# Cross-partition maxima, sums and score vectors of a four-layer graph kernel turned in 32 by 32 blocks on VectorE instead of on TensorE

## The reference, cut to what matters

```python
# x: [1354, 256], adj: [1354, 1354], all float32
x = layernorm(x + relu(adj @ (max(sign(x), 0) @ sign(W0).T)))        # L0: binary layer
# L1: edge layer
h = x @ W_sa
scores = (h @ a_sa[0, :256])[:, None] + (h @ a_sa[0, 256:])[None, :] # left scores, right scores
e = where(adj != 0, exp(-leaky_relu(scores, 0.01)), 0)
x = layernorm(x + sigmoid(attn_a * (e / (e.sum(1) + 1e-5)) @ h + attn_b * (adj @ (x @ W_gcn) + b)))
x = layernorm(x + (adj != 0) @ (x @ W + b) / deg)                    # L2: mean layer
y = x                                                                # L3: two softmax layers
for l in range(2):
    Wh, Ws = split(y @ W_stack[l])
    y = leaky_relu((softmax(Wh @ Ws.T, -1) * adj) @ Wh + y, 0.01)
out = layernorm(x + y)
```

## Time and profile before

| | |
|---|---|
| median of 3 runs | 483.96 us |
| the profiled execution | 483.51 us, of which 481.7 us is its span from first to last instruction |
| TensorE matmul busy | 471.0 us (98%), 1921 matmuls |
| VectorE busy | 349.7 us (73%) |
| ScalarE busy | 235.8 us (49%) |
| GpSimd busy | 187.4 us (39%) |
| granted TensorE clock, mean | 0.995 of full |

### The profile page before, as it was taken

The page is one execution under the profiler, slowest core; times in us unless marked ns, Lnnn a source line. Parts: engine busy times, 40 slices in busy tenths (PEclk is TensorE's granted clock), DMA queues, the critical chain, the costliest instruction groups (busy, mean ns, idle before and its releaser), DMA issues. The chain is left out here.

```text
span 481.7 us, 5723 instructions
## 1 busy us (share of the span) xinstructions
PE 471.0 (98%) x1921; PEld 310.7 (64%) x1921; DVE 349.7 (73%) x760; ACT 235.8 (49%) x417; POOL 187.4 (39%) x186
## 2 busy tenths in 40 slices
PE   8999999999999999999999999999999999999994
PEld 7999755545555688887545444554556545778882
DVE  5688799999955799748133953992853399799994
ACT  5979379973887553323434531341333376342200
POOL 1444654552352068823000631461440064356641
PEclk9999999999999999999999999999999999999998
DMA  8955310000544000000000000000000000000001
GB/s 293 291 164 178 128 33 1 0 1 0 181 165 150 1 1 0 1 0 1 1 0 0 0 1 1 1 1 0 0 0 1 0 2 1 1 11 23 22 23 39
DMA packets 8180, 20.69 MB, mean 43 GB/s; under 512 B 1008, under 2 KB 4740, under 8 KB 8152
## 3 DMA queue, kind: packets, MB, share of 16 engines
q1 hardware_dynamic: 7144, 19.02, 11.9%
q0 software_dynamic: 464, 0.79, 0.7%
q10 hardware_dynamic: 544, 0.52, 0.3%
HBM read 18.94 MB, written 1.39 MB: 42 GB/s over the span
## 5 line engine op out<-in xcount | busy, mean ns | idle before, releaser
L1505 PE MATMUL psum<-QT,xT 128*128 128x512 f32 (+3 forms) x264 | 108.5, 542 | 0.0
L427 POOL TENSOR_TENSOR es<-es,ST 128x512 f32<-128x512 f32 (+3 forms) x60 | 75.1, 1252 | 51.2 <-ACT ST L627 49.4
L622 ACT ACTIVATE ST<-psum 128x512 f32<-128x512 f32 (+3 forms) x66 | 36.1, 547 | 86.8 <-DVE rm L985 77.6
L1505 PEld LDWEIGHTS psum<-QT,xT 128*128 128x128 f32 (+1 forms) x264 | 47.7, 186 | 40.4 <-issue 34.0
L985 DVE TENSOR_TENSOR rm<-psum,rm 128x512 f32<-128x512 f32 (+3 forms) x60 | 37.4, 624 | 38.7 <-PE psum L1505 38.4
L365 POOL TENSOR_TENSOR rstd<-veps,nhalf 128x1 f32<-128x1 f32 (+1 forms) x44 | 29.3, 667 | 68.9 <-DVE veps L769 68.9
L1619 PE MATMUL psum<-Wh,ST 128*128 128x256 f32 (+3 forms) x242 | 55.1, 380 | 0.0
L1549 PE MATMUL psum<-ST,Wh 128*128 128x512 f32 (+3 forms) x132 | 54.5, 542 | 0.0
L1317 PE MATMUL psum<-eb,x_all 128*128 128x512 f32 (+3 forms) x132 | 51.9, 542 | 0.0
L627 ACT ACTIVATE ST<-ST 128x512 f32<-128x512 f32 (+3 forms) x66 | 37.9, 579 | 28.4 <-DVE ST L1007 25.5
L393 POOL TENSOR_TENSOR esumb<-esumb,eb 128x1354 f32<-128x1354 f32 (+1 forms) x10 | 32.4, 3236 | 46.8 <-ACT eb L515 46.8
(11 more groups left out here) (173 smaller groups left out, 779.3 us busy)
## 6 DMA issues: line engine op xcount, KB each, us to landing
adj_rows<-in_adj_dram SPq DMA_DIRECT2D x10, 677.0 KB, 4.9
rows<-in_adj_dram SPq DMA_DIRECT2D x10, 677.0 KB, 4.0
x_all<-in_x_dram SPq DMA_DIRECT2D x5, 256.0 KB, 4.7
out_dram<-xs SPq DMA_DIRECT2D x10, 128.0 KB, 1.7
W<-in_L_gnn_W_stack_dram SPq DMA_DIRECT2D x2, 512.0 KB, 6.3
adj_rows<-in_adj_dram SPq DMA_DIRECT2D x1, 338.5 KB
rows<-in_adj_dram SPq DMA_DIRECT2D x1, 338.5 KB
w0n<-in_L_gnn_weight_dram SPq DMA_DIRECT2D x1, 256.0 KB, 2.8
```

Of the source, the lines that this page charges most:

```text
L427: nc.gpsimd.tensor_tensor(es[0:r, g % 2, 0:w], es[0:r, g % 2, 0:w], buf(g)[0:r, j, 0:w], ALU.add)\
L622: nc.scalar.activation(buf(g)[0:r, j, 0:w], psum[0:r, SB[n % 3], 0:w], ACT.Copy).then_inc(st_ready.sem, 1)
L1505: last = nc.tensor.matmul(psum[0:r, SB[n % 3], 0:w], xT[l][:, k, j * P:j * P + r], QT[:, k, c0:c1], start=(k == 0), stop=(k == KD - 1))
```

## The change

Three spreads leave TensorE, for all but the last two groups.

- **Maxima of groups 0 to 3** (`max_blocks`): VectorE turns `rm` in 32 by 32 blocks, reduces each block, gathers the four quarters of partitions side by side with four small copies, reduces them, puts the result on the other three quarters with three copies, and turns a step-zero read of it straight into bank 7.
- **Denominators of groups 0 to 2** (`den_blocks`): the same with a sum and a reciprocal, ending in `rdb` in SBUF; ScalarE's copy goes too.
- **Left scores**: four copies gather `nsl` into `lefts`, three copies put it on the other quarters, and one block turn of a step-zero read of 1408 columns writes `nslb`; ScalarE's three copies go. They stand ahead of the right dot products.
- **`spread_dots`**: four transposes of step-zero reads of `ucol` replace eight matmul records of `Ub`; the memset and four adds of `Ub` go.

With them: ScalarE's `exp_scores(5)` moves behind the copies of `zT`; `z_proj` starts behind `h_part(2)` instead of `h_part(1)`, two for each `h_part` up to the fifth; the sums of group 1 lie in banks 5 and 6 instead of 2 and 3, so they no longer wait for `scale_t(0)`. `wh1(0)` waits for `scale_t(1)`.

```diff
+    SUMB = [2, 5, 2]
@@ ScalarE
-            for c, (c0, c1) in enumerate(CH):
-                act.wait_ge(left_spread.sem, c + 1)
-                nc.scalar.activation(nslb[:, c0:c1], bank(6 + c % 2, 0, c1 - c0), ACT.Copy).then_inc(nslb_ready.sem, 1)
...
-                exp_scores(j)
+                if j < RING - 1:
+                    exp_scores(j)
...
-                    if s == 0:
-                        rdb_evac(g)
@@ VectorE
             left_dot(T - 1)
+            dve.wait_ge(dots_done.sem, T)
+            for a in range(QUADS):
+                last = nc.vector.tensor_copy(lefts[0:BLOCK, :, a], nsl[a * BLOCK:(a + 1) * BLOCK, :])
+            own.link(last)
+            for a in range(1, QUADS):
+                last = nc.vector.tensor_copy(lefts[a * BLOCK:(a + 1) * BLOCK, :, :], lefts[0:BLOCK, :, :])
+            own.link(last)
+            nc.vector.transpose(nslb[:, :], lefts[:, :, :].rearrange("p t a -> p (t a)").unsqueeze(2).to_broadcast([P, T * QUADS, BLOCK]))\
+                .then_inc(nslb_ready.sem, 1)
...
+            def max_blocks(g):
+
+                w = chunk(g)[2]
+                nb = -(-w // BLOCK)
+                dve.wait_ge(rm_step.sem, T * (g + 1))
+                nc.vector.transpose(blocks[:, 0:nb * BLOCK], rm[:, g % 2, 0:nb * BLOCK]).then_inc(rm_blocked.sem, 1)
+                dve.wait_ge(rm_blocked.sem, g + 1)
+                own.link(nc.vector.tensor_reduce(quad[:, 0:nb], blocks[:, 0:nb * BLOCK].rearrange("p (b n) -> p b n", n=BLOCK), AX.X, ALU.max))
+                for a in range(QUADS):
+                    last = nc.vector.tensor_copy(gathered[:, a, 0:nb], quad[a * BLOCK:(a + 1) * BLOCK, 0:nb])
+                own.link(last)
+                own.link(nc.vector.tensor_reduce(quadmax[0:BLOCK, 0:nb], gathered[:, :, 0:nb].rearrange("p a b -> p b a"), AX.X, ALU.max,
+                                                 negate=True))
+                for a in range(1, QUADS):
+                    last = nc.vector.tensor_copy(quadmax[a * BLOCK:(a + 1) * BLOCK, 0:nb], quadmax[0:BLOCK, 0:nb])
+                own.link(last)
...
+                if g >= 1:
+                    dve.wait_ge(sub_done.sem, T * g)
+                nc.vector.transpose(psum[:, 7, 0:nb * BLOCK], quadmax[:, 0:nb].unsqueeze(2).to_broadcast([P, nb, BLOCK]))\
+                    .then_inc(spread_ready.sem, 1)
...
-                rden_cols(g)
+                den_blocks(g)
...
-            max_reduce(1)
+            max_blocks(1)
@@ TensorE
                 z_part(j)
-                if j == 1:
-                    for c in range(NC):
-                        spread_left(c)
...
-                for _ in range(2 if j <= 2 else 1):
-                    if i < T and j >= 1:
+                for _ in range(2 if j <= 5 else 1):
+                    if i < T and j >= 2:
                         z_proj(i)
                         i += 1
...
-                if j == T - LEAD_S:
-                    max_turn(1)
-                if j == T - 2:
-                    max_spread(1)
-            den(0)
             for s in range(LEAD_S):
                 s_tile(2, s)
-                if s == 0:
-                    spread_rden(0)
```

More of the change, by code:

```diff
@@ L528, in _ @@
             i = 0
+            exp_scores(RING - 1)
             for j in range(RING, T):
@@ L687, in _ @@
             q_evac(4)
-            wh1_evac(1)
-            rdb_evac(2)
-            for i in range(2, CROSS):
+            for i in range(1, CROSS):
                 wh1_evac(i)
@@ L1084, in _ @@
                 run_max(0, j)
-            max_reduce(0)
+            max_blocks(0)
             def both(g, s):
@@ L1109, in _ @@
                 both(0, s)
-            max_reduce(1)
+            max_blocks(1)
             turnover(0, T, 2)
-            max_reduce(2)
+            max_blocks(2)
             turnover(1, CROSS, 1)
@@ L1115, in _ @@
                 soft_step(2, s)
-            rden_cols(2)
+            den_blocks(2)
             scale_t(2)
@@ L1121, in _ @@
                 run_max(3, j)
-            max_reduce(3)
+            max_blocks(3)
             soft_step(3, 0)
@@ L1244, in spread_dots @@
                     for k in range(KD):
-                        last = nc.tensor.matmul(bank(0, half * D + k * P, half * D + (k + 1) * P), Ub[:, half, k, :],
-                                                ident[:, :], start=True, stop=True)
+                        last = nc.tensor.transpose(bank(0, half * D + k * P, half * D + (k + 1) * P), across(ucol[:, half, :], k, P), ident[:, :])
                 last.then_inc(ubc_ps.sem, 1)
@@ L1284, in z_part @@
                             last.then_inc(z_done.sem, 1)
-            def spread_left(c):
-                c0, c1 = CH[c]
-                if c == 0:
-                    pe.wait_ge(NA.x_ready.sem, T)
-                if c == 2:
-                    pe.wait_ge(nslb_ready.sem, 1)
-                for i in range(c0 // P, -(-c1 // P)):
-                    r = kk(i)
-                    pe.wait_ge(dots_done.sem, i + 1)
-                    last = nc.tensor.transpose(bank(6 + c % 2, i * P - c0, i * P - c0 + r), across(nsl, i, r), ident[0:r, 0:r])
-                last.then_inc(left_spread.sem, 1)
             def turn_exps(q):
@@ L1568, in den @@
                 last.then_inc(gat_den.sem, 1)
-            def spread_rden(g):
-                pe.wait_ge(rden_ready.sem, g + 1)
-                for n, i in enumerate(tiles(g)):
-                    r = kk(i)
-                    last = nc.tensor.transpose(bank(6, n * P, n * P + r), across(rden[:, g, :], n, r), ident[0:r, 0:r])
-                last.then_inc(rden_spread.sem, 1)
             def wh1(i):
@@ L1643, in _ @@
             q_mul(1)
-            max_turn(0)
             q_mul(2)
             s_tile(1, 0)
-            max_spread(0)
             for s in range(1, LEAD_S):
@@ L1666, in _ @@
                     s_tile(2, j + LEAD_S)
-                if j == T - LEAD_S:
-                    max_turn(2)
                 if j == T - 2:
-                    max_spread(2)
                     q_mul(3)
-            den(1)
             for s in range(LEAD_S):
                 s_tile(3, s)
-                if s == 0:
-                    spread_rden(1)
             for j in range(T):
@@ L1684, in _ @@
                     q_mul(4)
-            den(2)
-            wh1(1)
-            spread_rden(2)
-            for i in range(2, CROSS):
+            for i in range(1, CROSS):
                 wh1(i)
@@ L1692, in _ @@
             q_mul(5)
-            max_turn(3)
             wh1(CROSS)
             wh1(CROSS + 1)
-            max_spread(3)
             for j in range(T):
```

128 lines of the change are left out of this document (75 added, 53 removed).

## The result

The changed kernel takes 477.43 us (median of 4 runs, 477.12 to 478.37) for 484.01 us of the kernel before in the same comparison (4 runs, 483.92 to 484.13): a ratio of 0.9858, with 95% between 0.9841 and 0.9875. Its profiled execution took 477.23 us, of which 475.4 us is the span, for 483.51 and 481.7 before. The forecast was 477.1 with 475.5 to 480.5.

What follows compares the result with a forecast made beforehand. TensorE's streaming, busy 98% of the span, was taken as the bound. Six terms summed to 6.9 us off the profiled 483.51, giving 476.6; with 0.45 for the median, 477.1 us, range 475.5 to 480.5.

Steps and rivals of the forecast that it cites:

- left scores: Edge layer: TensorE loses its spread of the left scores, VectorE's added 3.1 us mostly hidden; gain 1.6 us, 0 to 1.5 at risk.
- spread_dots: Spreading in `spread_dots`: eight TensorE matmul records become four transposes; gain 0.4 us.
- seam of group 0: Behind group 0's last score tile: 8 transposes go, VectorE has 2.9 us in hand; gain 0.9 us.
- seam of group 1: The tight seam: 16 transposes go, but TensorE waits 0.9 to 1.5 us behind VectorE; gain 0.3 to 0.9, taken 0.5.
- seam of group 2: Behind group 2's last score tile: 14 transposes go, VectorE's 8.3 us fit in 12.0; gain 1.5 us.
- seam of group 3: `den(2)` with its spread, about 1.0, and group 3's maxima turn and spread, 1.0, leave TensorE; gain 2.0 us.
- Rival D: Whole kernel: the transposes were free and others set the pace, so nothing changes, 484.0 us; chance 0.04.
- C: Group 1 seam: VectorE not late, turns near 0.43 or copies near nothing; 1.2 us more gain, 475.5 to 475.9; chance 0.06.
- B: Group 1 seam: new wait outweighs the saving, slower; a turn of 1.65 us decides, 487.0 us at 2.0; chance 0.06.
- A: VectorE's new work: dear turns (1.26 us) or copies held by GpSimd; 480.7 us, with half of it 478.9; chance 0.18.
- the danger at `z_proj(8)`: Edge layer: `z_proj(8)` needs `zp_evac(6)`, queued on VectorE behind `scores(9)`; least cover left there about 1 us.
- The forecast's doubt: Left scores: GpSimd's `xp5` held VectorE's first score pass to 4.43 us; it would now meet the right dot products instead.

Runs made afterwards that it cites:

- e4: Changed kernel plus six redundant block turns on VectorE, two each in `max_blocks(0)`, `max_blocks(2)` and `den_blocks(1)`; 478.10 us.
- e6: Changed kernel with ScalarE's sixth exponential put ahead of the copies of `zT` again, as in the kernel before; 478.9 us.
- e5: Changed kernel with `z_proj` interleaved as in the kernel before, from `h_part(1)` on, two each up to j = 2; 477.84 us.
- e2: Changed kernel with the block sums of `den_blocks(0)` written to PSUM bank 5 and the four gathering copies reading from there; 477.41 us.
- e3: Changed kernel with two more redundant block turns of `es`, each waited for, in `den_blocks(0)`; 479.52 us.
- e8: The e3 kernel plus 20 transposes of the identity into a free PSUM bank on TensorE ahead of the waiting tile `s_tile(2, 3)`; 478.26 us.

## Why the prediction was right, and where its sum was off

Terms of the sum beside the stages, in us:

```
                   forecast   measured
left scores        1.6        1.67
spread_dots        0.4        about 0 in this execution
seam of group 0    0.9        0.88
seam of group 1    0.5        -0.09
seam of group 2    1.5        1.58
seam of group 3    2.0        2.25
sum                6.9        6.3
```

**Right, and shown.** That a transpose taken out of TensorE's full queue is worth its pace of 0.11 us: seams 0 and 2 come out within 0.1. That VectorE's block turn costs about a pass of its width: 0.70 to 0.73 for 0.69. That seam 1 is the only one where VectorE is late, that TensorE waits there for ScalarE's copy behind `run_max(2, 0)`, and that no wait appears at seams 0, 2, 3 (e4 shows that seams 0 and 2 had room for the turns of one block more). Rival D falls at once, C by the wait, B and the dear turns of A by the turns' length. The held copies of A came once, at seam 1, for 0.64; they were a sign of being wrong too ("if VectorE idles in front of copies while GpSimd runs"), and in the trace they show as a longer record (0.80 for 0.16) and not as idle time.

**Left scores.** Right in size, but with a gap in its reasons. The block took 59.06 + 1.65 - 57.49 = 3.2 us, as forecast (3.1), though made otherwise: the turn of 1408 columns was cheaper, 1.65 for 1.9, since its price doesn't grow quite with the columns (512 in 0.71, 1408 in 1.65), and the copies of `nsl` dearer, 0.2 each. The forecast looked for the danger at `z_proj(8)`; the first to suffer would have been the copies of `zT` behind an exponential on ScalarE (e6: 1.31 us). The forecast's doubt, that the hold-up by GpSimd "moves and is not new", was right for the first score pass (0.94 for 4.43) and misses that it can move to a pass that somebody waits for: the sixth tile's took 4.31 for 1.57. "What is queued behind the waiting instruction" had been asked for VectorE and not for ScalarE. The order of `z_proj` was worth another 0.6 (e5), so there was little cover.

**Seam of group 1, the step that failed.** The term was to be 0.3 to 0.9 with a wait of 0.9 to 1.5; it is -0.09 with 1.71. Three parts, all from VectorE's timeline. The hold of the copies by GpSimd was seen in the forecast (0.7) and came (0.64): that alone makes 0.3. I then took 0.5, a middle between holding and not holding, although the forecast's own schedule had the copies start inside GpSimd's addition: the hold is what is left of the addition when the first copy comes, and the schedule had given it. Second, the two blocks measure 3.79 (290.32 to 294.11) and, without the hold, 3.94 (295.31 to 299.89 less 0.64) for 3.6 and 3.8: the little reduction is 0.25 for 0.2, the reciprocal 0.24 for 0.2, and some of each. Together 0.19 + 0.14 = 0.33. Third, the restart of TensorE: 0.08, the fourth tile taking 302.17 - 300.98 = 1.19 until the next start for a pace of 1.11. 0.3 - 0.33 - 0.08 = -0.11, for -0.09 measured. A chain of ten or more small instructions, each rounded down by 0.03 to 0.05, is off by a third of a microsecond, and where the queue is on the path that all goes into the result.

**`spread_dots`.** Four matmuls fewer are there in TensorE's stream, but the start of z is at 53.88 for 53.91. In the changed kernel TensorE waits 0.6 us there for adjacency rows, which the kernel before didn't show, so what the four matmuls saved may have gone into waiting for a DMA. The stage moves by 2 us between executions, with the first DMAs and with the clock; 0.4 us can neither be confirmed nor refuted there, and no experiment was made for it.

**Seam of group 2.** The gain came as forecast, but one of its lengths was wrong: `den_blocks(1)` was put at 3.2, the length for the last chunk, while group 1 has 512 columns. VectorE's timeline of the changed kernel has its last turn, and what follows:

```profile
330.56 0.71 DVE L1066 STREAM_TRANSPOSE rdb<-quadsum 128x512 f32<-128x512 f32 x1
334.20 0.69 DVE L991 COPY rm<-psum 128x512 f32<-128x512 f32 x1 [2.93 <-PE psum L1544]
```

It began at 327.26 and so took 4.0, and the idle time of 2.93 behind it swallowed the difference; the slack there is 0.8 less than the 3.7 of the forecast.

**Seam of group 3.** 0.25 more than forecast, in two like parts. From `den(2)` to `s_tile(3, 8)` TensorE took 373.75 - 366.60 = 7.15 before and 6.04 after: 1.11 for "about 1.0". From `max_turn(3)` to `s_tile(4, 0)` it took 383.97 - 381.12 = 2.85 and 1.73: 1.12 for 1.0, of which the transposes are 0.88 and the rest a stop. In the kernel before, the eight matmuls of `wh1(8)` and `wh1(9)` between the earlier trace rows's `max_turn(3)` and `max_spread(3)` took 383.54 - 381.56 = 1.98; after the change the same eight stand thus (TensorE's timeline of the changed kernel):

```profile
375.94 1.89 PE L1615 MATMUL psum<-W,xT 128*128 128x256 f32 x8
377.67 1.88 PE L1544 MATMUL psum<-QT,xT 128*128 128x512 f32 x4
```

that is 1.73, so 0.25 of stop where the forecast had 0.12 of "small joints". `wh1(9)` writes bank 6 and had to wait there until `max_reduce(3)` had read the turned maxima (VectorE 381.76 to 382.45); the wait view leaves so short a stop out, but the distance of the starts shows it. The forecast should have looked at who else uses the bank that the removed step had occupied. That it was this wait is argued from the two timelines, not tried.

**The total.** 6.3 instead of 6.9 off the profile's span, and 477.4 instead of 477.1. Two errors of opposite sign (-0.6 and +0.25), and a term that can't be seen, lie in it. That the span came so near is in part luck: z starts at 53.91 and 53.88 in the two profiled executions, and would have been some 1.3 us apart had the clock fallen in one of them.

## What to carry to other kernels

Moving cross-partition work off a saturated TensorE pays its pace in full as long as the receiving engine's queue has nothing in it for which TensorE waits soon; cut the queue at that place and count every small instruction at its measured price, and put what isn't urgent (here the denominators) behind what is. When a producer gets later, go through every engine that waits for it and ask what is queued behind that wait: here the exponential on ScalarE, not the matmul that was guarded; ask too which passes of it now meet a neighbour that holds them. Compare stage by stage, by the starts of the same instructions, when the start of the program is noisier than the effect, and read the granted clock of the noisy stretch before calling it noise.

## What the runs showed of the hardware

- A VectorE block turn of f32 costs 0.70 to 0.73 us for 128 x 512, the same with a step-zero source and with PSUM as its target, and 1.65 for 128 x 1408.
- Four 32-partition copies of 16 columns take 0.69 us, 163 ns each, and 0.71 from PSUM. A copy from SBUF that began during GpSimd's addition lasted until its end (0.80 us); those from PSUM did not (e2), nor did block turns (0.71 to 0.74, e3). A long pass with both inputs in SBUF was held alike: 4.31 for 1.57 (e6).
- At the seam an idle stretch of 2.55 us of TensorE was followed by some 3 us at the lower clock, worth 1.68 us (e3); stretches of 1.7 were not, and neither was 0.37 behind 2.2 us of idle transposes (e8). A new wait thus costs in a step: 0.8 us more of waiting cost 2.5 us. But 1.7 us is not safe by itself: in the first stage, where several stops follow one another, the clock fell in the six executions whose longest stop was 1.18 to 1.78 us, and not in the seven with at most 1.08 (e8). What decides between the two places no run here shows.
- GpSimd's `xp5` and VectorE's dot products slow each other down instead of excluding each other: with `xp5` beside them, the dots came every 0.53 us for 0.35 elsewhere in the same kernel, and `xp5` took 6.22 us for 4.69 in the earlier trace rows. Beside GpSimd's sum of exponentials (105.80 to 108.84) a dot of the same kind took 3.26, to 0.29 behind its end. Before, `xp5` had met a score pass, which took 4.43 us; the first score pass now takes 0.94. VectorE's timeline of the changed kernel:

```profile
61.05 0.60 DVE L799 CUSTOM_DVE_ANT_0 dots<-x_all,ubc 128x256 f32<-128x256 f32 x1
61.58 0.08 DVE L799 DVE_READ_ACCUMULATOR2_ANT nsr<- 128x1 f32 x1
61.58 0.60 DVE L799 CUSTOM_DVE_ANT_0 dots<-x_all,ubc 128x256 f32<-128x256 f32 x1
...
66.50 0.94 DVE L853 TENSOR_SCALAR eb<-adjT 128x1354 f32<-128x1354 f32 x1
...
105.87 3.26 DVE L799 CUSTOM_DVE_ANT_0 dots<-x_all,wabc 128x256 f32<-128x256 f32 x1
```
